# Cross attention and a two-expert layer on one Trainium2 core: the eight-slot cycle laid out anew, and a three-pass second product

## The reference

```
h  = layernorm(x)                         # over the 256 columns
qk = einsum('bhdq,bhdl->bhql', h, ctx) / 4
x  = x + gamma * einsum('bhql,bhdl->bhdq', softmax(qk), ctx)
n  = layernorm(x)
e0 = gelu(n @ W0a.T + b0a) @ W0b.T + b0b  # exact gelu, 512 hidden units
e1 = relu(n @ W1a.T + b1a) @ W1b.T + b1b
x  = x + where(argmax(n @ Wg.T) == 0, e0, e1)
```

## Time and profile before

| | |
|---|---|
| median of 3 runs | 268.23 us (266.91 to 270.09) |
| the profiled execution, time / span | 267.05 us / 264.8 us |
| PE busy | 228.1 us (86%), 1858 matmul records |
| DVE busy | 167.5 us (63%) |
| ACT busy | 134.7 us (51%) |
| POOL busy | 63.9 us (24%) |
| mean granted TensorE clock | 0.972 of full speed |

### The profile page before, as it was taken

One profiled execution on the slowest core, in us unless ns is written; L12 is line 12 of the kernel. 1 busy time (PEld: TensorE's weight loads), 2 busy tenths in 40 slices (PEclk: granted clock), 3 DMA queues, 4 the chain that ended last, 5 costly groups with the idle time before them and its releaser, 6 DMA issues.

```text
span 264.8 us, 4862 instructions
## 1 busy us (share of the span) xinstructions
PE 228.1 (86%) x1858; PEld 172.2 (65%) x1872; DVE 167.5 (63%) x348; ACT 134.7 (51%) x208; POOL 63.9 (24%) x112
## 2 busy tenths in 40 slices
PE   0748947869599999999999999999999989989995
PEld 0425524444478676867686768676867676869893
DVE  3775687989635787578757875787476615333302
ACT  2014335665249454945494549554944494632230
POOL 6592120335700431043104310431101011011000
PEclk9999999798779999999999999999999999999999
DMA  4589999989712447375837582646202000000101
GB/s 158 85 156 165 207 289 171 253 165 153 102 22 80 101 136 110 100 107 123 116 101 102 125 117 62 99 97 108 64 0 64 0 22 2 20 22 0 40 2 40
DMA packets 19562, 25.75 MB, mean 97 GB/s; under 512 B 2644, under 2 KB 13140, under 8 KB 19284
## 3 DMA queue, kind: packets, MB, share of 16 engines
q1 hardware_dynamic: 18312, 24.25, 46.7%
q10 hardware_dynamic: 1228, 1.19, 2.1%
HBM read 11.28 MB, written 2.10 MB: 51 GB/s over the span
## 4 chain that ended last, share of the span: by engine, by line
PE 58%; ACT 17%; DVE 9%; DMA 7%; issue 7%; POOL 0%; SPq 0%; ACTq 0%; DVEq 0%
PE ff L740 21%; PE ff L723 12%; PE st L654 8%; DMA qkst<-mlow 6%; PE od L666 6%; ACT P L513 5%; ACT hid L542 4%; PE smax L642 3%; ACT L542 3%; PE st L629 2%; PE od L674 2%; ACT L513 2%; DVE nmax L351 2%; DVE y L423 1%; DVE yt L418 1%
## 5 line engine op out<-in xcount | busy, mean ns | idle before, releaser
L513 ACT ACTIVATE P<-st 128x1024 f32<-128x1024 f32 x64 | 65.8, 1028 | 85.4 <-PE st L654 76.9
L358 DVE TENSOR_REDUCE nmax<-smax 128x4 f32<-128x1024 f32 x54 | 66.2, 1226 | 40.2 <-PE smax L642 38.9
L740 PE MATMUL ff<-w2t,hid 128*128 128x256 f32 x256 | 60.0, 379 | 1.5 <-issue 1.1
L740 PEld LDWEIGHTS ff<-w2t,hid 128*128 128x128 f32 x256 | 47.7, 190 | 5.8
L723 PE MATMUL ff<-xnTh,w1h 128*128 128x256 f32 x128 | 39.1, 306 | 9.0 <-DVE y L423 3.4
L239 POOL TENSOR_TENSOR mv<-mv,power 128x1 f32<-128x1 f32 x31 | 18.3, 591 | 103.8 <-DVE mv L323 103.8
L654 PE MATMUL st<-qkst 50*128 50x256 f32 x240 | 31.2, 339 | 9.1 <-DMA qkst<-mlow 5.5
L723 PE MATMUL ff<-xnTl,w1h 128*128 128x256 f32 x128 | 37.1, 290 | 0.0
L723 PE MATMUL ff<-xnTh,w1l 128*128 128x256 f32 x128 | 37.1, 290 | 0.0
L654 PEld LDWEIGHTS st<-qkst 50*128 50x128 f32 x240 | 18.5, 191 | 26.2 <-issue 14.4
L666 PE MATMUL od<-P,vt 128*32 128x256 f32 x512 | 33.5, 406 | 0.0
(11 more groups left out here) (73 smaller groups left out, 250.9 us busy)
## 6 DMA issues: line engine op xcount, KB each, us to landing
qkst<-parts SPq DMA_DIRECT2D x87, 128.0 KB, 4.7
xv<-in_xv SPq DMA_DIRECT2D x16, 256.0 KB, 2.9
qk<-in_qk SPq DMA_DIRECT2D x15, 256.0 KB, 4.6
out<-y SPq DMA_DIRECT2D x16, 128.0 KB, 2.4
w1t<-in_w SPq DMA_DIRECT2D x1, 1024.0 KB, 10.2
w2t<-in_w SPq DMA_DIRECT2D x1, 1024.0 KB, 9.9
qkst<-parts ACTq DMA_DIRECT2D x3, 128.0 KB, 6.2
qk<-in_first SPq DMA_DIRECT2D x1, 256.0 KB, 3.4
```

The source lines that it names most:

```text
L358: dve.tensor_reduce(nmax[:, c % 2, :, :, j].rearrange("p a e -> p e a"), (ff if c in WIDE and j % 2 else smax)[:, :, :, :], AX.X, ALU.max, ...
L513: act.activation(P[:, b % 2, j, :, :, :].rearrange("p e a l -> p (e a l)"), st[:, :, :, :].rearrange("p e a l -> p (e a l)"), ACT.Exp, sca ...
L740: mm = pe.matmul(ff[:, t, u // HM, :], hid[:, u, t * C:(t + 1) * C], w2t[:, u, :], start=False, stop=u == UNITS - 1)
```

## The change

- **Slots.** `values(b-1)` moves from slot 1 to slot 0 of batch b, ahead of the second `scores`; everything behind it moves with it: `transpose_od` from slot 3 to slot 1, `transpose_att` and the residual from slot 0 of the next batch to slot 2 of the same, `x_norm` and `gate` from slot 1 of the next batch to slot 3, `transpose_x` from slot 2 to slot 0 of the next batch. `normalise` stands first in DVE's slot 2.
- **First product.** gemm1 of pair i goes from slots 0 and 2 of batch 2i+4 to slots 1, 2 and 3 of batch 2i+3 (4, 2 and 2 hidden tiles). The first one stands in batch 3 and no longer in batch 4, and no gemm1 but the last pair's stands behind the loop. The split of its weights on POOL (`w1l`) goes from batch 3 to slots 2 and 3 of batch 2.
- **Second product.** For batches 0 to 13 gemm2 is three passes of float32r instead of one float32 matmul: `high_pass` (hidH with w2h and w2l) and `low_pass` (hidL with w2h), per expert. hidH is copied by DVE for the gelu half (`high_gelu`) and by ACT for the relu half (`high_relu`), hidL by POOL for both (`low_hidden`, two instructions of 128x1024 per pair). The weights are split once: w2h on ACT in slots 0 and 1 of batch 3, w2l on POOL in slots 2 and 3 of batch 3. Batches 14 and 15 keep the float32 form.
- `low` on POOL stands two slots later, where its input is ready; `x1` has 6 buffers and not 8.

```diff
@@ -43,7 +45,7 @@
 XV = 4
-X1 = 8
+X1 = 6
@@ -256,6 +262,12 @@
+            def low_hidden(i, e):
+                pool.wait_ge((s_hidHg, s_hidHr)[e], i + 1)
+                units = slice(e * HM, (e + 1) * HM)
+                pool.tensor_tensor(hidL[:, units, :], hid[:, units, :], hidH[:, units, :], ALU.subtract).then_inc(s_hidL, 1)
@@ -290,25 +302,33 @@
                 b, j = divmod(n, PAIRS)
+                if b >= 4 and j == 0 and b % 2 == 0:
+                    low_hidden((b - 4) // 2, 1)
...
                         rstd(c, mv1, c, s_var1, s_rstd1)
+                for c in prepared(n - 2 if n > 0 else n) if n else ():
...
                     continue
-                if j == 2 and b + 1 < B:
+                if j == 1 and b + 1 < B:
                     pad_values(b + 1)
-                if j == 0 and b >= 2:
-                    rstd(b - 2, mv2, b - 1, s_var2, s_rstd2)
-                if j == 2 and b >= 2:
-                    masks(b - 2)
-                if b == 3 and j < LC:
-                    pool.wait_ge(s_w1h, j + 1)
-                    pool.tensor_tensor(w1l[:, j, :, :], w1t[:, j, :, :], w1h[:, j, :, :], ALU.subtract).then_inc(s_w1l, 1)
-            rstd(B - 2, mv2, B - 1, s_var2, s_rstd2)
-            masks(B - 2)
+                if j == 2 and b >= 1:
+                    rstd(b - 1, mv2, b, s_var2, s_rstd2)
+                if j == 3 and b >= 1:
+                    masks(b - 1)
+                if b >= 3 and j == 3 and b % 2:
+                    low_hidden((b - 3) // 2, 0)
+                if b == 2 and j >= 2:
+                    pool.wait_ge(s_w1h, j - 1)
+                    pool.tensor_tensor(w1l[:, j - 2, :, :], w1t[:, j - 2, :, :], w1h[:, j - 2, :, :], ALU.subtract).then_inc(s_w1l, 1)
+                if b == 3 and j >= 2:
+                    pool.wait_ge(s_w2h, j - 1)
+                    half = slice((j - 2) * HM, (j - 1) * HM)
+                    pool.tensor_tensor(w2l[:, half, :], w2t[:, half, :], w2h[:, half, :], ALU.subtract).then_inc(s_w2l, 1)
+            low_hidden(B // 2 - 2, 1)
@@ -410,6 +430,12 @@
                 dve.tensor_tensor(xnTl[here], tr[:, 0, :, :], xnTh[here], ALU.subtract).then_inc(s_xTl, 1)
+            def high_gelu(i):
+                dve.wait_ge(s_hid, UNITS * i + HM)
+                if i:
+                    dve.wait_ge(s_g2, 2 * i)
+                dve.tensor_copy(hidH[:, 0:HM, :], hid[:, 0:HM, :]).then_inc(s_hidHg, 1)
@@ -457,11 +483,15 @@
                 c, k = divmod(n + LEAD, PAIRS)
+                if j == 1 and b >= 5 and b % 2:
+                    final(b - 4)
+                if j == 2 and b >= 1:
+                    normalise(b - 1)
...
                     take_max(c, k)
-                if (k == 0 and b < 4 or k == 1 and b >= 4) and 2 <= c <= B:
+                if k == 0 and 2 <= c <= B:
@@ -470,24 +500,17 @@
                 if j == 0 and b >= 2:
-                    if b >= 6 and b % 2 == 0:
-                        final(b - 5)
-                    residual(b - 2)
-                    moments2(b - 2)
-                if j == 1 and b >= 2:
-                    x_norm(b - 2)
-                    gate(b - 2)
+                    low_xT(b - 2)
+                if j == 2 and b >= 1:
+                    residual(b - 1)
+                    moments2(b - 1)
                 if j == 3 and b >= 1:
-                    normalise(b - 1)
-                    if b >= 2:
-                        low_xT(b - 2)
-                if j == 2 and b >= 5 and b % 2:
-                    final(b - 5)
-            residual(B - 2)
-            moments2(B - 2)
-            final(B - 5)
-            x_norm(B - 2)
-            gate(B - 2)
+                    if b >= 3 and b % 2:
+                        high_gelu((b - 3) // 2)
+                    x_norm(b - 1)
+                    gate(b - 1)
+                    if b >= 4 and b % 2 == 0:
+                        final(b - 4)
@@ -534,11 +557,20 @@
+            def high_relu(i):
+                act.wait_ge(s_hid, UNITS * (i + 1))
+                if i:
+                    act.wait_ge(s_g2, 2 * i)
+                act.activation(hidH[:, HM:UNITS, :], hid[:, HM:UNITS, :], ACT.Copy).then_inc(s_hidHr, 1)
...
                     act.wait_ge(s_g1, UNITS // 2 * i + u // 2 + 1)
-                if u == 0 and i:
-                    act.wait_ge(s_g2, 2 * i)
+                if u % HM == 0 and 0 < i < LAST:
+                    act.wait_ge(s_hidL, EXPERTS * (i - 1) + u // HM + 1)
+                if u == 0 and i == LAST:
+                    act.wait_ge(s_hidL, EXPERTS * LAST)
@@ -574,29 +606,31 @@
                     act.activation(w1h[:, j, :, :], w1t[:, j, :, :], ACT.Copy).then_inc(s_w1h, 1)
+                if b == 3 and j < EXPERTS:
+                    act.wait_ge(s_w2, 16)
+                    half = slice(j * HM, (j + 1) * HM)
+                    act.activation(w2h[:, half, :], w2t[:, half, :], ACT.Copy).then_inc(s_w2h, 1)
...
                     copy_max(c - 1)
-                if j == 1 and b >= 4:
-                    if b % 2 == 0:
-                        if b == 4:
+                if j == 0 and b >= 2:
+                    high_xT(b - 2)
+                    if b >= 4 and b % 2 == 0:
+                        high_relu((b - 4) // 2)
+                if j == 1 and b >= 1:
+                    copy_od(b - 1)
+                    if b >= 3 and b % 2:
+                        if b == 3:
...
                         for u in range(4):
-                            hidden((b - 4) // 2, u)
-                if j == 2 and b >= 1:
-                    copy_od(b - 1)
-                    if b >= 4 and b % 2 == 0:
-                        for u in range(4, 8):
-                            hidden((b - 4) // 2, u)
-                if j == 3 and b >= 2:
-                    high_xT(b - 2)
-            for u in range(4):
-                hidden(B // 2 - 2, u)
+                            hidden((b - 3) // 2, u)
+                if j >= 2 and b >= 3 and b % 2:
+                    for u in range(2 * j, 2 * j + 2):
+                        hidden((b - 3) // 2, u)
+            high_xT(B - 2)
+            high_relu(B // 2 - 2)
             copy_od(B - 1)
-            high_xT(B - 2)
-            for u in range(4, 8):
-                hidden(B // 2 - 2, u)
@@ -725,22 +759,42 @@
-            def gemm2(b, units):
+            def begin(b):
                 t = b % 2
-                if 0 in units:
-                    if b == 0:
-                        pe.wait_ge(s_w2, 16)
-                        pe.wait_ge(s_bias, 7)
-                        pe.wait_ge(s_ones, 2)
-                    pe.wait_ge(s_hid, UNITS * (b // 2) + (UNITS if t else UNITS - 2))
-                    pe.matmul(ff[:, t, :, :], onesb[:, :], bias_rows[:, :], start=True, stop=False)
-                for u in units:
+                if b == 0:
+                    pe.wait_ge(s_w2, 16)
+                    pe.wait_ge(s_bias, 7)
+                    pe.wait_ge(s_ones, 2)
+                pe.wait_ge(s_hid, UNITS * (b // 2) + (UNITS if t else UNITS - 2))
+                pe.matmul(ff[:, t, :, :], onesb[:, :], bias_rows[:, :], start=True, stop=False)
+            def high_pass(b, e):
+                t = b % 2
+                pe.wait_ge((s_hidHg, s_hidHr)[e], b // 2 + 1)
+                if b == 0:
+                    pe.wait_ge(s_w2l, EXPERTS)
+                for u in range(e * HM, (e + 1) * HM):
+                    for w in (w2h, w2l):
+                        pe.matmul(ff[:, t, e, :], hidH[:, u, t * C:(t + 1) * C], w[:, u, :], start=False, stop=False)
+            def low_pass(b, e):
+                t = b % 2
+                pe.wait_ge(s_hidL, EXPERTS * (b // 2) + e + 1)
+                for u in range(e * HM, (e + 1) * HM):
+                    mm = pe.matmul(ff[:, t, e, :], hidL[:, u, t * C:(t + 1) * C], w2h[:, u, :],
+                                   start=False, stop=u == UNITS - 1)
+                if e == EXPERTS - 1:
+                    mm.then_inc(s_g2, 1)
+            def gemm2(b):
+                t = b % 2
+                begin(b)
+                for u in range(UNITS):
...
                                    w2t[:, u, :], start=False, stop=u == UNITS - 1)
-                if UNITS - 1 in units:
-                    mm.then_inc(s_g2, 1)
+                mm.then_inc(s_g2, 1)
@@ -757,52 +811,66 @@
                 if k == 0 and 2 <= c <= B:
-                    transpose_max(c - 1, max(0, b - 2))
+                    transpose_max(c - 1, max(0, b - 1))
                 even = b >= 4 and b % 2 == 0
-                odd = b >= 5 and b % 2
+                odd = b >= 3 and b % 2
...
                     if b >= 2:
-                        transpose_att(b - 2)
+                        transpose_x(b - 2, b + 1)
+                    if b >= 1:
+                        if b == 1:
+                            pe.wait_ge(s_vones, 2)
+                        values(b - 1)
+                    if odd and b >= 5:
+                        high_pass(b - 4, 1)
```

(64 more changed lines are left out.)

13 lines of the change are left out of this document (9 added, 4 removed).

## The result

The changed kernel takes 271.19 us (median of 19 runs, 270.21 to 274.03), the kernel before on the same chip 269.14 (266.91 to 270.93): a ratio of 1.0102, 95% interval 1.0073 to 1.013. It is 1% slower. Forecast were 263 us and a range of 255 to 269. The profiled execution took 272.31 us with a span of 270.4.

What follows compares the result with a forecast made beforehand. PE's list was taken as the bound from batch 5 on, a path through other engines before it. 89 + 106.4 + 24.5 + 40.1 gave a 260.0 us span, 263 us on the median's scale, range 255 to 269.

Steps and rivals of the forecast that it cites:

- the startup: Stretch up to the first `scores` of batch 5: +2.3 us in sum, from 86.54 to about 89 (87 to 93).
- Batch 1, +1.9: Startup: second `scores` come 2.85 us after the first instead of 1.7, more at half clock; 1.9 us longer.
- Batch 2, +1.5: Startup: the same later second `scores`, values and `transpose_x` now ahead of slot 1; 1.5 us longer.
- Batch 3, +6.3: Startup: batch 3 gets a gemm1, 5.7 us, and a wait on `w1l`, 0.6; added to its 9.4.
- Batch 4, -7.4: Startup: gemm1 and its `w1l` wait gone from 20.0 us; content 10.6 plus a 2 us wait for w2l, 12.6.
- The second product, 8.4 us: gemm2 of 14 batches on PE: three passes take 3.04 us instead of 3.64, 8.4 us less in all.
- The cycle, 26.6: Batches 5 to 12: content 23.7 us plus waits of 0.6, 0.6, 1.35 and 0.4; unchanged at 26.6.
- the lock: Port pair shared exclusively by DVE and POOL: `x_norm` stands still behind `low`; cycle 26.6 us, without it 25.3.
- Last cycle and end: Batches 13 and 14 take 24.5 us against 26.50; from batch 15 on 40.1 against 45.25.
- 1 (no lock): Cycle of batches 5 to 12: `x_norm` gets in before `low`, cycle 25.3, time 256.5 us; chance 0.22.
- 2 (startup at 93): Startup ruled by the maxima's rows and POOL's queue, half clock; batch 5 at 93, time 267 us; chance 0.16.
- 3 (clock falls in every cycle): Batches 5 to 12: the wait at `transpose_x` lowers the clock, four cycles +9.8, time 273 us; chance 0.12.

Runs made afterwards that it cites:

- e4: Changed kernel with `transpose_x` behind values instead of ahead of it in slot 0 of every batch; 267.66 us, ratio 0.9875 to the kernel before.
- e5: Changed kernel with the splits of both weights (w1h, w1l, w2h, w2l) half a batch earlier; 265.87 us, ratio 0.9873 to the kernel before.
- e6: Changed kernel with `transpose_x` behind values and the splits of both weights half a batch earlier; 261.22 us, ratio 0.9701 to the kernel before.
- e11: Changed kernel with only the split of the second weights (w2h, w2l) half a batch earlier; 268.05 us, ratio 0.9957 to the kernel before.
- e9: Kernel of e6 with the second product in float32 again, without its casts and splits; 267.71 us, ratio 0.9932 to the kernel before.
- e1: Changed kernel with POOL's `low` behind `masks` in slot 3 from batch 1 on; 271.10 us, ratio 1.0040 to the kernel before.
- e7: Changed kernel with unread filler transposes on PE in startup waits: 32, 14 and 8 in batches 1, 2 and 3; 270.00 us, ratio 1.0009.
- e12: Kernel of e6 with 24 unread filler transposes ahead of the first `scores` of batch 1; 260.21 us, ratio 0.9675 to the kernel before.
- e3: Changed kernel with values back in slot 1 for batches below 4; 273.64 us, ratio 1.0137 to the kernel before.
- e10: Kernel of e6 with POOL's `low` behind `masks`; 261.71 us, ratio 0.9721 to the kernel before.

## Why the prediction was wrong, point by point

**The failed step is the startup**: "Sum: 1.9 + 1.5 + 6.3 - 7.4 = +2.3; batch 5 starts at about 89". It is +11.9, of which +10.9 lie in the batches. Its terms:

- *Batch 1, +1.9*: measured +1.28. Right in kind; one execution's scatter is of the same size.
- *Batch 2, +1.5*: measured +5.12. I priced the longer way to the second `scores` by PE's content alone, 2.85 us. In the cycle I had found that `transpose_x`, now ahead of values, waits for `x_norm`; in the startup I didn't look for it, and the sum has no term for it. There it is 2.08 us, and with it values at half rate, then `exp`, the copy of w1h and the copy of `od` one behind the other. e4 (transpose behind values) took 2.4 of batch 2, e5 (w1's split earlier) 1.8, both 3.6.
- *Batch 3, +6.3*: measured +8.33. A wait of 1.16 for `x_norm`, which POOL's `w1l` made 2.04 us long, and values at 3.09 instead of 1.86. Both repairs together took 1.0. What holds the rest is not shown: in e6 values of this batch still take 3.43, and PE waits 1.00 for `take_max` (63.15) and 0.78 for `exp` (75.80; 1.37 at 80.05 in the changed kernel).

```profile
65.80 2.04 DVE L417 TENSOR_SCALAR xn<-x,mv 128x256 f32<-128x256 f32 x1
```

```profile
65.34 2.35 POOL L326 TENSOR_TENSOR w1l<-w1t,w1h 128x1024 fp32r<-128x1024 f32 x1
```

- *Batch 4, -7.4, with "a wait: 2 us" for w2l*: measured -3.87. The wait was right, 2.20. What was missing is the wait for `x_norm`, 1.16, the half rate behind the wait for w2l, some 1.5 us, and 0.6 us of content: an even batch of the cycle takes 12.16, of which 0.92 are waited, and I had 10.6. The 1.5 are an estimate: the 3.97 us that e11 takes from batch 4, less 2.20 for the wait and 0.24 by which the wait for `x_norm` is shorter in the cycle.

Taken together, e6 moves batch 5 to 89.90 and the time to 261.22 with two moves of order and no other work: that is the forecast's startup (89) and close to its sum (262.3 for such an execution; e6's took 261.96). The sum is met by luck in part: against the forecast e6 has +0.9 at batch 5, -2.4 in four cycles, and +1.3 and +0.3 in the last cycle and the end. But most of the miss is shown by experiment: 8.6 of the 9.5 us by which batch 5 came late.

**The second product, 8.4 us**: right in kind, mis-sized. 6.5 by e9 against e6. Matmuls do stand 0.12 apart (90.14 to 90.86 in the changed kernel), but I left out most of what the changes between operations cost, as 0.20 from the first of a group to the second (89.94 to 90.14). One batch's three passes with their bias matmul take 3.36 in the changed kernel (149.79 to 151.54 and 154.45 to 156.06), where I had 3.04; in float32 they take 3.76 in e9 (162.86 to 164.80 and 166.49 to 168.31), where I had 3.64.

**The cycle, 26.6**: measured 26.53, but by two errors that cancel, which is luck. The waits were over-costed: forecast 1.35 + 0.4 for `x_norm`, measured 0.92 in the even batches and none in the odd ones; `exp` 0.6, measured 0.54; `transpose_att` 0.3 each, measured 0.2 (in the changed kernel it starts at 147.21 where `maxima`, from 146.67, would let it start at 147.01; DVE's division ends at 147.15). The content was under-costed: 26.53 less these 1.9 us is 24.7, not 23.7, and e1's 25.94 less its waits (0.54, 0.4 and the 0.26 for `low_hidden`) is 24.7 too. The price of the lock in a cycle is 0.92 as a wait and 0.59 as e1 could win it back, not 1.3.

**Last cycle and end**: 25.21 for 24.5 and 40.59 for 40.1. Near, both somewhat too low; that the same missing content is behind it is argued, not shown.

**The rivals.** 1 (no lock) fell: `x_norm` took 1.37, and 0.41 once `low` was moved. 2 (startup at 93) was the nearest in kind, and had 6.5 of the 11.9 us. Its half clock in the startup came about (0.50 at 52.93 to 56.51). Its path fell: the first `scores` of batches 2 to 4 never waited for the maxima's rows; the waits were for `x_norm`, ACT, POOL, and once 0.54 for `take_max`. 3 (clock falls in every cycle) fell: 1.00 in all 106.13 us, though PE waited 0.92 us four times. The slower side came about, but in the startup, where the clock was low before the change too (0.86, now 0.80).

What stays open: how much of batches 2 and 3 is half clock that a busier PE would get rid of (e7 won 0.9 and 0.4 there, e12 only batch 1); what else makes batch 3 long; and why e3's batch 3 grew.

## What to carry to other kernels

A wait that you find in the steady cycle is to be looked for in the startup too, where the same order stands and the engines behind it have the one-time work as well: one operation ahead of values cost 0.5 us in a cycle and over 2 us in one batch of the startup. An operation that waits for another engine belongs behind those whose inputs are old; that made the lock free, without taking it away. And one-time splits go earlier: half a batch earlier they no longer stood on two queues in front of what PE waited for. A wait that is taken away can reappear at the next thing that is late: in e1 and e4 PE came sooner to `w2l` and waited longer for it.

## What was not expected of the hardware

- An instruction of POOL that asked while DVE was at its cast went ahead of DVE's next one: `low` at 165.81, `x_norm` at 166.15, ended 167.52 (shown above; e1 and e10 without it 0.41).
- A cast of 128x1024 to float32r on DVE took 0.68 us, against 0.42 for one of 512 to bfloat16: twice the elements in 1.6 times the time.
- Half rate in values of one batch costs 1.7 us: 3.64 in the changed kernel and 1.93 behind e7's fillers for the same 32 matmuls. The wait of 4.53 us did not bring it on: ahead of it four `maxima` took 0.59 (31.58 to 32.17) and not 0.34. The fillers got PE out of it: 24 took 4.80 us (e12), eight more only 0.68 (e7's 5.48). The row of the granted clock has 1.00 from the start to 45.3 us, so there it and the distances disagree. Behind waits of 0.92 in the cycle the clock did not fall.
- The runs of one kernel differ with the clock: those of the changed kernel at a mean of 0.962 took 270.2 to 271.0 us, at 0.949 to 0.950 272.6 to 274.0. Which of the two follows the other these runs don't show.
